# The local-attention loop of a two-block model on one core: three engines' order inside an iteration, and where the l2 norm's bound is applied

## The chip, the cores and the metric

One core of a Trainium2 chip runs the whole program. The engines each take their instructions in the order in which the program lists them, and wait for each other through semaphores: TensorE (PE in the profile, its weight loads apart as PEld), VectorE (DVE), ScalarE (ACT), GpSimd (POOL) and SyncE (SP), which here only issues DMAs. The metric is the device time of one launch in microseconds (us), the median of the runs.

## The reference, cut to what matters

The model takes `x` of 8 sequences x 256 tokens x 128 channels through ten residual steps. The change touches the two-layer local-attention block, which stands among them twice. All data is fp32.

```python
def _layer(x, wqkv, qs, ksc, wo, lg, lb, w1, b1, w2, b2):     # DIM 128, HEADS 8, DIM_HEAD 64, WINDOW 64
    h = shift_token(x)                                         # half of the channels from the token before
    q, k, v = jnp.split(h @ wqkv, 3, axis=-1)
    q, k, v = (to_heads(q), to_heads(k), to_heads(v))
    q = l2norm(q) * qs                                         # t / clip(norm(t), 1e-12)
    k = l2norm(k) * ksc
    q, k = rotary_xpos(q, k)
    o = local_attention(q, k, v)                               # own window and the one before, softmax
    x = x + o.transpose(0, 2, 1, 3).reshape(b, n, INNER) @ wo
    h = shift_token(x)
    h = (h - mu) / jnp.sqrt(var + 1e-05) * lg + lb             # layer norm
    a, g = jnp.split(h @ w1 + b1, 2, axis=-1)                  # 2 x 341 hidden units
    h = a * jax.nn.gelu(g, approximate=False)
    return x + h @ w2 + b2
...
for l in range(2):
    x = _layer(x, wqkv[l], q_scale[l], k_scale[l], wo[l], ...)
...
x = x + _L1_ffn_ref(_layernorm(x, axis=-1), ...)               # stands twice, with _L1_attn_b_ref between
```

## The kernel before, in words

A batch is 256 tokens, held as two tiles (`t` = 0, 1) of 128 tokens on the partitions. The local block is a loop over 2 layers x 8 batches, run twice (the first and the second block below). One iteration, `win(n, l, i)`, does three things at once: the attention of batch `i` (four units `u` of 64 query tokens and all 8 heads), the projections of the next batch (`nxt`: queries, keys, their rotation and norms, values), and pieces of the MLP of earlier batches (`hid` is batch i-1, whose layer norm is made, `m` is batch i-2, whose two matmul stages are made). The first two iterations of a block have no `m`, the first no `hid` either; the last has no `nxt`. So a block has 2 light iterations, 13 full ones with `nxt`, and the last. In the first block's second layer the iterations with `m` also normalise the finished batch for the next step (`fin`: `final_stats`, `norm_apply`); the second block needs no such norm.

Each engine's part of `win` is one list written by hand, and that list is what the engine does in order. The steps that the prediction follows:

- PE: `transpose_x` (the next batch's shifted tokens, which POOL copied to `xst`), `project_qk(t)` (queries and keys of tile t into two banks), `hidden_gates`, `hidden_values`, `hidden_out` (MLP), `local_scores(u)`, `transpose_probs(u)`, `weigh_values(u)`, `project_values(t)`, `transpose_qk(t)`, and `project_out`, the last step.
- ACT: `shifted` (the transposed tokens to `hT`), `gelus` between two table switches (`prime`), `squares(t)`, `local_exp(u)`, copies out of PSUM.
- DVE: `attn_max(u)`, `weigh(u)` (a reciprocal and a product), `rope_part(t, m)` (rotation of the queries, m = 0, and the keys, m = 1; the last one of a tile releases POOL's sum), `norms(t)` (sum of squares per head, then a `tensor_scalar` that bounds it from below by 1e-24), `hidden_stats` (mean and variance for the layer norm, ending in the small `tensor_scalar` at L1089 that writes `hvar`), `hidden_apply` (four `tensor_scalar`s of 128x64, L1096 and L1097), `gated`, `mlp_end`, `scaled(t)` (rotated values times the inverse norm, L999), and `local_residual`, which waits for `project_out`.
- POOL, unchanged in its order by the diff: `stage_copy` (L548, writes `xst`), the rotation's sum of tile 0 (L556, 128x1024), the inverse norms of tile 0 (L552, a power), `hidden_rstd`, with `m` in layer 1 `final_add`, the sum and the inverse norms of tile 1, and with `fin` the `final_rstd`, before the next `stage_copy`.

Of the kernel before, what the change touches and what calls it, by code (L numbers as in the profile page):

```python
# [26 lines left out]
P = 128  # L27
# [62 lines left out]
def attn_unit(u, groups):  # L90

    if u < groups:
# [29 lines left out]
        "dve_chain": F_UNITS, "ssq_chain": NT, "stage_ready": 1, "xT_psum": 1, "xT_ready": 1, "qk_psum": NT, "sq_ready": NT,  # L123
# [94 lines left out]
def build(nc, x, out, consts, w, plan):  # L218
    with ExitStack() as ctx:
# [242 lines left out]
        def _(pool):  # L462
# [68 lines left out]
            for n, kind in enumerate(plan):  # L531
# [22 lines left out]
                def rope_pool(v, i, t):  # L554
                    pool.wait_ge(sems["rope_ready"], v.at("rope_ready", i, t + 1))
                    pool.tensor_tensor(t1[:, t], t1[:, t], t2[:, t], ALU.add).then_inc(sems["rope_sum"], 1)  # L556
                    inverse_norms(v, i, t)

# [11 lines left out]

                def local_step(n, l, i):
                    _, nxt, m, hid = around(n, l, i)
                    fin = m and m[0] is vals[n + 3]
                    if nxt:
                        stage_copy(nxt[1], n + 2 * nxt[2])
                        rope_pool(nxt[0], nxt[1], 0)
# [4 lines left out]
                    if nxt:  # L581
                        rope_pool(nxt[0], nxt[1], 1)
# [81 lines left out]
        def _(dve):  # L664
# [323 lines left out]
            def norms(v, i, t, ch):  # L988

                dve.wait_ge(sems["sq_ready"], v.at("sq_ready", i, t + 1))
                ch.link(dve.tensor_reduce(ssq[:, t], sq[:, t].rearrange("p (h d) -> p h d", d=FHD), AX.X, ALU.add))
                dve.tensor_scalar(ssq[:, t], ssq[:, t], 1e-24, None, ALU.max).then_inc(sems["ssq_ready"], 1)  # L993

            def scaled(v, i, t):
# [3 lines left out]
                dve.tensor_tensor(qk[:, t].rearrange("p (h d) -> p h d", d=FHD), t1[:, t].rearrange("p (h d) -> p h d", d=FHD),  # L999
                                  inv[:, t].broadcast_to([P, 16, FHD]), ALU.mult).then_inc(sems["qk_ready"], 1)  # L1000

            def win_open(v, l, t):

                norms(v, 0, t, Chain(dve, v, "ssq_chain", 0, t))
# [8 lines left out]
            def win(n, l, i):  # L1013
# [4 lines left out]
                if nxt:  # L1018
                    vn, ni, nl = nxt
                    sch = Chain(dve, vn, "ssq_chain", ni)  # L1020
# [20 lines left out]
                weigh(0)  # L1041
                if m:
                    gated(*m)
# [4 lines left out]
                if m:  # L1048
# [1261 lines left out]
```

## Time and profile before

| | |
|---|---|
| median of 3 runs | 1893.99 us (1893.68 to 1896.01) |
| the profiled execution | 1894.08 us; from its first to its last instruction 1891.9 us |
| busy share of that span | PE 84%, DVE 70%, PEld 67%, ACT 59%, POOL 24% |
| granted TensorE clock, mean | 0.925 of full speed |
| first block's loop | 615.12 to about 1068 us |
| second block's loop | 1438.92 to about 1885 us |

An engine's busy share is an average over stages that have different limits. An iteration of the loop begins where PE transposes the staged tokens (line 2041 of the kernel before), so two starts of that line give its length.
### The profile page before, as it was taken

To read this page: it belongs to the slowest core of one execution; us is meant where nothing else is said; L and a number is where in the kernel's file an instruction comes from. 1 tells how busy PE (TensorE), PEld (TensorE's weight loads), DVE (VectorE), ACT (ScalarE), POOL (GpSimd) and SP (SyncE) were. 2 spreads that over 40 slices of the span, in tenths; PEclk is the share of its full clock that TensorE was granted. 3 is DMA by queue.
4 is the path that set the end of the run, shared out by engine and by line. 5 is a ranking of instruction groups with operands and counts; after the bars stand their busy time and mean duration, and the time that the engine had idled before them with its cause. 6 is when DMAs were issued, how large, how long until landed. Compare 5 with 4: busy or idle time off the path is not lost.

```text
span 1891.9 us, 31365 instructions
## 1 busy us (share of the span) xinstructions
PE 1587.9 (84%) x9787; PEld 1268.3 (67%) x9787; DVE 1333.8 (70%) x3495; ACT 1116.8 (59%) x2975; POOL 454.2 (24%) x342
## 2 busy tenths in 40 slices
PE   6999989766555789889878799999986889888986
PEld 5888888334344567776667677777764667766775
DVE  4678877788985777877776555565646877887783
ACT  2355455233221788888777743443425888888885
POOL 1110010000002443434444100000004443434450
PEclk9999999677677999999999999998998999999999
DMA  4000000000010000000000000000000000000000
GB/s 144 1 1 0 0 0 1 1 1 1 1 56 0 2 4 3 1 4 4 2 3 1 4 1 0 0 0 0 0 1 1 4 3 3 2 4 4 3 1 25
DMA packets 15110, 13.49 MB, mean 7 GB/s; under 512 B 11286, under 2 KB 14266, under 8 KB 14650
## 3 DMA queue, kind: packets, MB, share of 16 engines
q1 hardware_dynamic: 15034, 12.55, 2.1%
q8 instruction: 38, 0.62, 0.1%
q14 instruction: 38, 0.31, 0.1%
HBM read 9.41 MB, written 1.05 MB: 6 GB/s over the span
## 4 chain that ended last, share of the span: by engine, by line
PE 59%; DVE 18%; issue 11%; ACT 9%; POOL 2%; DVEq 0%; POOLq 0%; ACTq 0%
PE bank L1740 5%; PE bank L1715 5%; PE bank L1752 4%; PE bank L1681 4%; PE bank L1701 4%; PE bank L1879 3%; PE bank L1727 3%; PE bank L1766 3%; PE bank L1861 2%; DVE arena_ffn L984 2%; PE bank L1883 2%; PE bank L1692 2%; PE bank L1899 2%; PE bank L1956 2%; DVE hvar L1089 2%
## 5 line engine op out<-in xcount | busy, mean ns | idle before, releaser
L556 POOL TENSOR_TENSOR arena_ffn<-arena_ffn 128x1024 f32<-128x1024 f32 x60 | 141.5, 2358 | 397.3 <-DVE arena_ffn L984 397.3
L552 POOL TENSOR_TENSOR inv<-ssq,mhalf 128x16 f32<-128x16 f32 x64 | 188.1, 2940 | 67.9 <-DVE ssq L993 64.4
L1437 ACT ACTIVATE bank<-bank,nmaxF 128x128 f32<-128x128 f32 x512 | 173.3, 340 | 49.7 <-DVE nmaxF L717 48.9
L1367 ACT ACTIVATE prob<-bank,nmax 128x128 f32<-128x128 f32 (+1 forms) x256 | 90.1, 420 | 114.9 <-DVE nmax L717 90.5
L1715 PEld LDWEIGHTS bank<-arena_setup 128*128 128x128 f32 x1024 | 146.1, 206 | 10.2 <-issue 1.3
L1727 PE MATMUL bank<-ident,prob 128*128 128x128 f32 x512 | 83.9, 290 | 79.9 <-DVE prob L1028 55.0
L1727 PEld LDWEIGHTS bank<-ident,prob 128*128 128x128 f32 x512 | 63.1, 148 | 122.8 <-issue 100.9
L1715 PE MATMUL bank<-arena_setup 128*128 128x128 f32 x1024 | 145.2, 288 | 0.0
L540 POOL TENSOR_TENSOR rstd<-var,mhalf 128x2 f32<-128x2 f32 x24 | 17.0, 709 | 524.2 <-DVE var L679 524.2
L1752 PE MATMUL bank<-packF,hT 128*128 128x512 f32 x256 | 130.9, 637 | 11.5 <-DVE arena_ffn L984 9.8
L717 DVE TENSOR_REDUCE nmaxF<-bank 128x4 f32<-128x512 f32 x128 | 88.4, 691 | 70.2 <-PE bank L1715 70.1
L1388 ACT ACT_TABLE_LOAD x91 | 116.8, 1283 | 1.6
L980 DVE TENSOR_TENSOR arena_ffn<-bank,rope 128x512 f32<-128x512 f32 x128 | 87.5, 683 | 32.2 <-ACT arena_attn L1415 32.2
L1740 PE MATMUL bank<-probT,vF 128*128 128x128 f32 x768 | 101.9, 282 | 4.7 <-ACT probT L1444 4.3
L1437 ACT ACTIVATION_READ_ACCUMULATOR bank<-bank,nmaxF 128x1 f32 x512 | 105.2, 205 | 0.4
L1456 ACT ACTIVATE arena_setup<-bank 64x256 f32<-64x256 f32 x256 | 96.2, 376 | 10.7 <-PE bank L1740 9.1
L1681 PE MATMUL bank<-arena_attn 128*128 128x256 f32 (+1 forms) x512 | 100.0, 328 | 0.0
L1841 PE MATMUL bank<-xqT,w1s 128*114 128x256 f32 (+1 forms) x384 | 97.3, 390 | 1.8 <-ACT arena_forget L1475 0.7
L1740 PEld LDWEIGHTS bank<-probT,vF 128*128 128x128 f32 x768 | 90.7, 191 | 11.8 <-issue 6.9
L984 DVE TENSOR_TENSOR arena_ffn<-bank,rope 128x256 f32<-128x256 f32 x256 | 95.4, 414 | 0.0
L1141 DVE TENSOR_TENSOR arena_forget<-bank,maskG 128x384 f32<-128x384 f32 x128 | 68.1, 552 | 38.5 <-PE bank L1901 35.0
L1415 ACT ACTIVATE arena_attn<-bank 128x512 f32<-128x512 f32 x128 | 69.5, 599 | 43.1 <-PE bank L1752 43.1
(271 smaller groups left out, 4128.3 us busy)
## 6 DMA issues: line engine op xcount, KB each, us to landing
packF<-in_packF SPq DMA_DIRECT2D x1, 3122.0 KB
arena_history<-in_packG SPq DMA_DIRECT2D x1, 2560.0 KB, 9.8
HS<-XH SPq DMA_DIRECT2D x32, 63.5 KB
X<-in_x_tiled SPq DMA_DIRECT2D x1, 1024.0 KB, 4.9
out_dram<-X SPq DMA_DIRECT2D x8, 128.0 KB, 1.9
arena_setup<-in_const_masks_a SPq DMA_DIRECT2D x1, 512.0 KB, 5.5
HS<-XH SPq DMA_DIRECT2D x32, 0.2 KB
arena_setup<-in_const_rope SPq DMA_DIRECT2D x1, 256.0 KB
```

The source lines that it names most:

```text
L552: pool.tensor_tensor(inv[:, t, :, 0], ssq[:, t, :, 0], mhalf[:, 0:16], ALU.pow).then_inc(sems["inv_ready"], 1)
L556: pool.tensor_tensor(t1[:, t], t1[:, t], t2[:, t], ALU.add).then_inc(sems["rope_sum"], 1)
L984: ins = dve.tensor_tensor(heads(t2[:, t, cols])[:, :, d], a[:, :, e], tab, ALU.mult)
L1388: act.activation(primer[:, col:col + 1], mhalf[:, 0:1], func)
L1437: ins = act.activation(cols, cols, ACT.Exp, bias=nmaxF[:, u, c:c + 1], accum_out=denF[:, u, c])
L1456: ins = act.activation(yTF[rows_, u // 2, :, 64 * (u % 2):64 * (u % 2) + 64], bank[6 + u % 2][rows_].rearrange("p (c j k) -> p c j k", j=2 ...
L1681: ins = pe.matmul(bank[s % banks][:, n * width:(n + 1) * width], q, k, start=False, stop=True, skip_group_check=True)
L1715: ins = pe.matmul(b[:, c * P:(c + 1) * P].rearrange("p (a k) -> p a k", a=2), qZ[:, u, c].rearrange("p j k -> p (j k)"), kT[:, c, F_KEYS[u ...
L1727: ins = pe.transpose(bank[4 + u % 2][:, c * P:(c + 1) * P], prob[:, u % 2, c * P:(c + 1) * P], ident[:])
L1740: ins = pe.matmul(bank[6 + u % 2][:, c * P:(c + 1) * P], values[:, c * P:(c + 1) * P], probT[:, u % 2, c * P:(c + 1) * P], start=True, sto ...
L1752: ins = pe.matmul(bank[banks[m]][:], hT[:, t * P:(t + 1) * P], f_at[f"wqkv{l}"][:, 512 * m:512 * m + 512], start=True, stop=True)
L1841: return pe.matmul(dst, w1s[:, l, lo:lo + n], xqT[:], start=True, stop=True)
```

## The change

The bound moves: `norms` no longer has the `tensor_scalar` that bounds the sum of squares, and `scaled` becomes a `scalar_tensor_tensor` that bounds the inverse norm from above by 1e12 in the same pass. The remaining edits give the engines' steps in an iteration another order. POOL's functions are split in two, with the same order of instructions.

```diff
             def norms(v, i, t):
                 dve.wait_ge(sems["sq_ready"], v.at("sq_ready", i, t + 1))
-                ch.link(dve.tensor_reduce(ssq[:, t], sq[:, t].rearrange("p (h d) -> p h d", d=FHD), AX.X, ALU.add))
-                dve.tensor_scalar(ssq[:, t], ssq[:, t], 1e-24, None, ALU.max).then_inc(sems["ssq_ready"], 1)
+                dve.tensor_reduce(ssq[:, t], sq[:, t].rearrange("p (h d) -> p h d", d=FHD), AX.X, ALU.add).then_inc(sems["ssq_ready"], 1)
...
-                dve.tensor_tensor(qk[:, t].rearrange("p (h d) -> p h d", d=FHD), t1[:, t].rearrange("p (h d) -> p h d", d=FHD),
-                                  inv[:, t].broadcast_to([P, 16, FHD]), ALU.mult).then_inc(sems["qk_ready"], 1)
+                dve.scalar_tensor_tensor(qk[:, t].rearrange("p (h d) -> p h d", d=FHD), inv[:, t].broadcast_to([P, 16, FHD]), 1e12,
+                                         t1[:, t].rearrange("p (h d) -> p h d", d=FHD), ALU.min, ALU.mult).then_inc(sems["qk_ready"], 1)
...
+                scaled(v, i, 1)
                 attn_max(v, i, 0, 4, P, nmaxF, F_SCORE_BANKS)
-                scaled(v, i, 1)
                 if nxt:
                     rope_part(vn, ni, nl, 0, 0)
-                attn_max(v, i, 1, 4, P, nmaxF, F_SCORE_BANKS)
-                if nxt:
-                    rope_part(vn, ni, nl, 0, 1)
+                if m:
+                    gated(*m)
                 if hid:
                     hidden_stats(*hid)
                 if nxt:
-                    norms(vn, ni, 0, sch)
+                    rope_part(vn, ni, nl, 0, 1)
+                attn_max(v, i, 1, 4, P, nmaxF, F_SCORE_BANKS)
                 weigh(0)
+                if nxt:
+                    norms(vn, ni, 0)
                 if m:
-                    gated(*m)
+                    mlp_end(m[0], m[1])
                 weigh(1)
...
                 weigh(3)
-                if nxt:
-                    norms(vn, ni, 1, sch)
                 if hid:
                     hidden_apply(*hid)
                 if nxt:
-                    scaled(vn, ni, 0)
-                local_residual(v, i, l)
+                    norms(vn, ni, 1)
                 if fin:
                     final_stats(m[0], m[1])
+                if nxt:
+                    scaled(vn, ni, 0)
+                if fin:
                     norm_apply(m[0], m[1])
+                local_residual(v, i, l)
...
                 if m:
                     prime(ACT.Gelu)
+                    gelus(*m)
                 if nxt:
                     squares(vn, ni, 0)
                 if m:
-                    gelus(*m)
                     prime(ACT.Exp, 1)
                 local_exp(v, i, 0)
+                middle_values(v, i)
                 take_qkT(v, i, 1)
                 local_exp(v, i, 1)
...
                     transpose_x(vn, ni, bank[2])
-                local_scores(v, i, 0)
-                if nxt:
-                    project_qk(vn, ni, nl, 0)
                 if m:
                     hidden_gates(*m, 0)
                     pe.wait_ge(sems["down_used"], v.at("down_used", i, 0))
                     hidden_gates(*m, 1)
-                local_scores(v, i, 1)
+                if nxt:
+                    project_qk(vn, ni, nl, 0)
+                local_scores(v, i, 0)
                 if m:
                     hidden_values(*m)
                 transpose_qk(v, i, 1)
+                local_scores(v, i, 1)
+                if m:
+                    hidden_out(*m)
                 if nxt:
                     project_qk(vn, ni, nl, 1)
+                local_scores(v, i, 2)
                 transpose_probs(v, i, 0)
-                local_scores(v, i, 2)
-                if m:
-                    hidden_out(*m)
                 local_scores(v, i, 3)
                 transpose_probs(v, i, 1)
```

The lists of PE and ACT also change near the end of an iteration (`project_values(1)` earlier, `weigh_values(3)` behind the hidden transpose, one copy of ACT's moved).

DVE, the end of a full iteration (the batch before the last of layer 0), before: `weigh(3)`, then the sum of squares and its bound, `hidden_apply` on `hn`, the scaling and the residual.

```order
L980 TENSOR_TENSOR arena_ffn<-bank,rope 128x512
L984 TENSOR_TENSOR arena_ffn<-bank,rope 128x8x32 x2
L1025 RECIPROCAL rdenF<-denF 128x4
L1028 TENSOR_TENSOR prob<-bank,rdenF 128x512
L992 TENSOR_REDUCE ssq<-arena_attn 128x16
L993 TENSOR_SCALAR ssq<-ssq 128x16
L1096 TENSOR_SCALAR hn<-XH,mv,hrstd 128x64
L1097 TENSOR_SCALAR hn<-HS,mv,hrstd 128x64
L1096 TENSOR_SCALAR hn<-XH,mv,hrstd 128x64
L1097 TENSOR_SCALAR hn<-HS,mv,hrstd 128x64
L999 TENSOR_TENSOR arena_attn<-arena_ffn,inv 128x1024
L1071 TENSOR_TENSOR XH<-XH,bank 128x256
```

The same place now.

```order
L981 TENSOR_TENSOR arena_ffn<-bank,rope 128x512
L985 TENSOR_TENSOR arena_ffn<-bank,rope 128x8x32 x2
L1024 RECIPROCAL rdenF<-denF 128x4
L1027 TENSOR_TENSOR prob<-bank,rdenF 128x512
L1094 TENSOR_SCALAR hn<-XH,mv,hrstd 128x64
L1095 TENSOR_SCALAR hn<-HS,mv,hrstd 128x64
L1094 TENSOR_SCALAR hn<-XH,mv,hrstd 128x64
L1095 TENSOR_SCALAR hn<-HS,mv,hrstd 128x64
L993 TENSOR_REDUCE ssq<-arena_attn 128x16
L999 SCALAR_TENSOR_TENSOR arena_attn<-inv,arena_ffn 128x1024
L1069 TENSOR_TENSOR XH<-XH,bank 128x256
```

`hidden_apply` has moved ahead of the sum of squares, the bound has gone, and the scaling stands right behind the sum of squares.

PE, the start of a full iteration of the rolled loop, before (`xst` is the staged batch, `hT` its transposed tokens, `xqT` the MLP's input):

```order
L2041 MATMUL bank<-ident,xst 128x128
L2042 MATMUL bank<-ident,xst 128x128
L1712 MATMUL bank<-maskFb,identb 128x512
L1715 MATMUL bank<-arena_setup 128x128 x4
L1752 MATMUL bank<-packF,hT 128x512 x2
L1841 MATMUL bank<-xqT,w1s 114x256 x2
L1841 MATMUL bank<-xqT,w1s 113x256
```

The same place now.

```order
L2040 MATMUL bank<-ident,xst 128x128
L2041 MATMUL bank<-ident,xst 128x128
L1840 MATMUL bank<-xqT,w1s 114x256 x2
L1840 MATMUL bank<-xqT,w1s 113x256
L1750 MATMUL bank<-packF,hT 128x512 x2
L1710 MATMUL bank<-maskFb,identb 128x512
L1713 MATMUL bank<-arena_setup 128x128 x4
```

The gates of the MLP now stand between the transposes and the projection, and the scores of unit 0 behind the projection.

## Rows read from the trace of the kernel before

**Rows 1.** Loop stretches: us, busy (x instructions) of PE, PEld, DVE, ACT, POOL; clock, DMA.

```profile
615.12:668.09 52.97, 42.37 (x263) 32.19 (x263) 36.75 (x74) 39.90 (x124) 23.34 (x11) 0.94 0.01 2
668.09:887.27 219.18, 196.79 (x1250) 156.39 (x1249) 170.17 (x384) 188.30 (x545) 92.43 (x48) 0.98 0.01 3
887.27:1061.84 174.57, 145.58 (x900) 117.36 (x898) 124.92 (x316) 136.29 (x399) 65.98 (x41) 0.94 0.01 3
1491.77:1818.31 326.54, 292.93 (x1875) 232.29 (x1873) 255.07 (x576) 282.49 (x817) 141.53 (x76) 0.98 0.01 3
```

**Rows 2.** PE in time order, one full iteration: start, duration, line [idle before <-releaser].

```profile
1709.35 0.27 PE L2041 MATMUL bank<-ident,xst 128*128 128x128 f32 x1
...
1710.98 1.89 PE L1752 MATMUL bank<-packF,hT 128*128 128x512 f32 x4
...
1715.10 1.46 PE L1841 MATMUL bank<-xqT,w1s 128*114 128x256 f32 x6
...
1721.99 0.65 PE L1727 MATMUL bank<-ident,prob 128*128 128x128 f32 x4 [2.70 <-DVE prob L1028]
...
1734.48 1.95 PE L1773 MATMUL bank<-packF,arena_setup 128*128 128x128 f32 x16
1736.26 0.27 PE L2041 MATMUL bank<-ident,xst 128*128 128x128 f32 x1
```

**Rows 3.** DVE in time order, the same iteration.

```profile
1717.18 0.22 DVE L1082 BATCH_NORM_STATS2 stats<-XH 128x6 f32 x1
...
1718.28 1.43 DVE L1089 TENSOR_SCALAR hvar<-mv 128x2 f32<-128x2 f32 x1 [0.17 <-DVE mv L1087]
1719.62 1.21 DVE L992 TENSOR_REDUCE ssq<-arena_attn 128x16 f32<-128x1024 f32 x1
...
1721.78 1.26 DVE L1110 SCALAR_TENSOR_TENSOR arena_forget<-bank,b1s,arena_forget 114x256 f32<-114x256 f32 x3
1722.96 0.17 DVE L1025 RECIPROCAL rdenF<-denF 128x4 f32<-128x4 f32 x1
...
1723.79 0.69 DVE L717 TENSOR_REDUCE nmaxF<-bank 128x4 f32<-128x512 f32 x1
1724.40 0.68 DVE L980 TENSOR_TENSOR arena_ffn<-bank,rope 128x512 f32<-128x512 f32 x1
...
1725.66 0.41 DVE L1116 TENSOR_TENSOR XH<-XH,bank 128x256 f32 x1
...
1731.39 0.30 DVE L1096 TENSOR_SCALAR hn<-XH,mv,hrstd 128x64 f32 x1
...
1732.28 1.21 DVE L999 TENSOR_TENSOR arena_attn<-arena_ffn,inv 128x1024 f32<-128x1024 f32 x1
```

**Rows 4.** POOL in time order, the same iteration.

```profile
1717.34 2.35 POOL L556 TENSOR_TENSOR arena_ffn<-arena_ffn 128x1024 f32<-128x1024 f32 x1 [9.45 <-DVE arena_ffn L984]
...
1731.55 2.91 POOL L552 TENSOR_TENSOR inv<-ssq,mhalf 128x16 f32<-128x16 f32 x1
1734.42 0.40 POOL L548 COPY xst<-XH 128x256 f32 x1
```

**Rows 5.** All engines in time order, the head of a `fin` iteration.

```profile
948.01 0.33 PE L2041 MATMUL bank<-ident,xst 128*128 128x128 f32 x1 [2.65 <-POOL xst L548]
```

**Rows 6.** All engines in time order, just behind the first block's loop.

```profile
1077.31 0.72 POOL L565 TENSOR_TENSOR X<-X,XH 128x256 f32<-128x256 f32 x1
1077.37 0.71 DVE L1096 TENSOR_SCALAR hn<-XH,mv,hrstd 128x64 f32<-128x64 f32 x1 [0.59 <-POOL hrstd L561]
```

**Rows 7.** All engines in time order, end of the first block's first iteration.

```profile
637.07 1.21 DVE L999 TENSOR_TENSOR arena_attn<-arena_ffn,inv 128x1024 f32<-128x1024 f32 x1
637.23 3.82 POOL L552 TENSOR_TENSOR inv<-ssq,mhalf 128x16 f32<-128x16 f32 x1
```

**Rows 8.** All engines in time order, an earlier stage of the program.

```profile
265.16 1.04 POOL L520 TENSOR_TENSOR taps<-ident,arena_setup 128x512 f32<-128x512 f32 x1
265.26 0.24 DVE L793 RECIPROCAL qrecip<-qscale 128x16 f32<-128x16 f32 x1
```

More of the change, by code:

```diff
@@ L122 @@
     "win": {
-        "dve_chain": F_UNITS, "ssq_chain": NT, "stage_ready": 1, "xT_psum": 1, "xT_ready": 1, "qk_psum": NT, "sq_ready": NT,
+        "dve_chain": F_UNITS, "stage_ready": 1, "xT_psum": 1, "xT_ready": 1, "qk_psum": NT, "sq_ready": NT,
         "v_psum": NT, "v_ready": NT,
@@ L569, in final_rstd, with rope_sum @@
                     pool.tensor_tensor(rstd[:], var[:], mhalf[:, 0:NT], ALU.pow).then_inc(sems["rstd_ready"], 1)
+                def rope_sum(v, i, t):
+                    pool.wait_ge(sems["rope_ready"], v.at("rope_ready", i, t + 1))
+                    pool.tensor_tensor(t1[:, t], t1[:, t], t2[:, t], ALU.add).then_inc(sems["rope_sum"], 1)
                 def local_step(n, l, i):
-                    _, nxt, m, hid = around(n, l, i)
+                    v, nxt, m, hid = around(n, l, i)
                     fin = m and m[0] is vals[n + 3]
@@ L575, in local_step @@
                         stage_copy(nxt[1], n + 2 * nxt[2])
-                        rope_pool(nxt[0], nxt[1], 0)
+                        rope_sum(nxt[0], nxt[1], 0)
+                        inverse_norms(nxt[0], nxt[1], 0)
                     if hid:
@@ L581, in local_step @@
                     if nxt:
-                        rope_pool(nxt[0], nxt[1], 1)
+                        rope_sum(nxt[0], nxt[1], 1)
+                        inverse_norms(nxt[0], nxt[1], 1)
                     if fin and m[0] is not vals[-1]:
@@ L986, in rope_part, with norms @@
                     ins.then_inc(sems["rope_ready"], 1)
-            def norms(v, i, t, ch):
+            def norms(v, i, t):
                 dve.wait_ge(sems["sq_ready"], v.at("sq_ready", i, t + 1))
-                ch.link(dve.tensor_reduce(ssq[:, t], sq[:, t].rearrange("p (h d) -> p h d", d=FHD), AX.X, ALU.add))
-                dve.tensor_scalar(ssq[:, t], ssq[:, t], 1e-24, None, ALU.max).then_inc(sems["ssq_ready"], 1)
+                dve.tensor_reduce(ssq[:, t], sq[:, t].rearrange("p (h d) -> p h d", d=FHD), AX.X, ALU.add).then_inc(sems["ssq_ready"], 1)
             def scaled(v, i, t):
@@ L1047, in win @@
                     rope_part(vn, ni, nl, 1, 0)
-                if m:
-                    mlp_end(m[0], m[1])
                 attn_max(v, i, 3, 4, P, nmaxF, F_SCORE_BANKS)
@@ L1498, in win @@
                     squares(vn, ni, 1)
-                middle_values(v, i)
+                probs_copy(v, i, 0)
                 local_exp(v, i, 2)
-                probs_copy(v, i, 0)
                 probs_copy(v, i, 1)
@@ L1506, in win @@
                 take_yT(v, i, 1)
+                take_yT(v, i, 2)
                 probs_copy(v, i, 3)
-                take_yT(v, i, 2)
                 if hid:
@@ L1820, in win @@
                     project_values(vn, ni, nl, 0)
+                weigh_values(v, i, 2)
                 transpose_probs(v, i, 3)
-                weigh_values(v, i, 2)
-                weigh_values(v, i, 3)
+                if nxt:
+                    project_values(vn, ni, nl, 1)
                 if hid:
@@ L1826, in win @@
                     transpose_hidden(hid[0], hid[2])
+                weigh_values(v, i, 3)
                 if nxt:
-                    project_values(vn, ni, nl, 1)
                     transpose_qk(vn, ni, 0)
```

10 lines of the change are left out of this document (1 added, 9 removed).

## The prediction

> **What bounds the kernel now.** I read the windows of the loop first, then PE, DVE and POOL in time order over one iteration, then the places elsewhere in the trace where POOL and DVE overlap. By the windows the loop makes an iteration in about 27 us: eight full ones take 219.18, twelve take 326.54, the two light ones at a block's head 52.97, and the stretch with `fin` 174.57 [rows 1]. A full iteration in which nothing slows TensorE lasts from 1709.35 to 1736.26, 26.91 us [rows 2]. 8 x 26.91 = 215.3 and 12 x 26.91 = 322.9, so 3.9 and 3.6 us are left, with the granted clock at 0.98 in both windows. The only pause of PE in [rows 2] that is longer than about a microsecond is the 2.70 ahead of the first transposes of probabilities, and I take the falls of the clock to come behind it.
>
> That pause ends with `weigh(0)` on DVE. [Rows 3] show what DVE did before: the small `hvar` instruction on 128x2 took 1.43, and then the sum of squares took 1.21. The 1.43 isn't its own work. POOL's sum of tile 0 ran from 1717.34 for 2.35, to 1719.69 [rows 4], and `hvar` ended at 1719.71. So a `tensor_scalar` on DVE that comes under POOL's 128x1024 sum is held until that sum ends. The same is seen on the form of `hidden_apply`: 0.71 instead of 0.30 under a POOL addition of 0.72 that had begun 0.06 earlier [rows 6, 3]. It also goes the other way: POOL's power, 2.91 alone [rows 4], takes 3.82 when it is issued 0.16 behind the scaling on DVE, 0.91 more [rows 7]. But a scaling that starts when the power already runs is not held: 1.21 at 1732.28, inside the power of 1731.55 [rows 3, 4]. There are 28 such scalings, all 1.21.
>
> At the end PE is the last: the staged copy is done at 1734.82 [rows 4], the output projection runs from 1734.48, and the next iteration starts at 1736.26 [rows 2]. In a `fin` iteration it is the other way, PE waits 2.65 for the copy [rows 5], because POOL must first make the final norm's power.
>
> **The change part by part.** Times below count from PE's start of the iteration.
>
> *Head.* On PE the same three steps (projection, gates, scores) stand ahead of the second rotation, in another order. In [rows 2] they take 15.10 - 10.98 = 4.12. With the two transposes (0.22, an estimate from the 0.27 of one) the scores of unit 0 are ready at about 4.5, and `attn_max(0)` ends at 5.15, which is the first thing that DVE has to wait for; the ACT squares, no longer behind two table switches, are ready at about 4.9 by my walk.
>
> *DVE from there runs without a pause.* Start to start in [rows 3]: a rotation 1.26 (24.40 to 25.66), the gated product 1.18 (21.78 to 22.96), `weigh` 0.83 (22.96 to 23.79), a maximum 0.61 (23.79 to 24.40), the sum of squares 1.21, `mlp_end` 0.41, the statistics 1.10 with `hvar` at 0.1 now that POOL's sum isn't running. `hvar` comes ahead of the second rotation, so POOL's sum starts behind it: 1.3 saved. Until the last rotation releases POOL's second sum DVE does four rotations (5.04), the product (1.18), the statistics (1.2), three maxima (1.83), three weighings (2.49), one sum of squares (1.21) and `mlp_end` (0.41): 13.4, so 18.5.
>
> *The tail, where it is lost again.* POOL's sum runs 18.5 to 20.85 (2.35, [rows 4]). DVE does `weigh(3)` and issues `hidden_apply` at 19.3. Before, the sum of squares stood there and hid POOL's sum; now four `tensor_scalar`s come under it, and by the 1.43 and the 0.71 the first is held to 20.85: 1.5 lost where `hvar` gained 1.3. The other three take 0.22 each ((32.28 - 31.39)/4 in [rows 3]) and end at 21.5. The sum of squares ends at 22.7. The bound that is gone would have been 0.2 to 0.3 here. `scaled(0)` needs nothing that is late, so DVE issues it at 22.65, just ahead of the power at 22.75: that is the arrangement of [rows 7], so the power takes 3.82 and not 2.91, to 26.5. The copy (0.40, [rows 4]) ends at 26.9. PE: scaling ends 23.8, eight transposes about 0.9 (half of the sixteen matmuls of 1.79 between 1734.48 and 1736.26), the projection 1.79: 26.5. So the copy becomes last, at 26.9: a full iteration keeps its 26.9. The bound's own 0.2 goes to nothing: it lay on DVE ahead of a power that now starts no earlier.
>
> The scaling as one `scalar_tensor_tensor` has no row of its own size. Below, it costs the 1.21 of the product; above, the L1110 form costs 0.39 per 256 columns start to start, 1.57 for 1024 columns. I take 1.21; +0.36 on PE's path would still end at 26.9.
>
> *What is gained.* (a) The 2.70 pause: `weigh(0)` now stands ahead of the sum of squares, and `hidden_out` and the second projection stand in PE's list before the transposes. By the walk PE's longest pauses are about 1.1. If the falls of the clock go with the pause, the 3.9 and the 3.6 go, and 1.4 in the rest: -9. (b) `fin` iterations: the final statistics (about 1.0, like `hidden_stats`) now stand between the sum of squares and the scaling, so the power starts alone and takes 2.91: 25.65, the final power 0.7 (an estimate between 0.40 and 2.91), copy 0.40: 26.75. PE: scaling 1.0 later, 24.8, transposes 0.9, projection 1.79: 27.4. Before, the five of them with projections take 30.5 each (174.57 less 22 for the last batch's part, by five): -3.1 each, -15.5, and some 1.5 of the last batch's: -17. (c) Light iterations: 52.97 for two. The same walk without the product and `mlp_end` is 1.6 shorter, 25.3; without the statistics (1.2) and the held `hidden_apply` too, the first would be 23 or 24, where PE's and ACT's own steps bind. Together 49.2, -3.7 in each block. As I can't walk the waits for ACT well there, I take -3 in each: -6.
>
> Sum: 0 - 9 - 17 - 6 = -32. The profiled execution's own time is 1894.08, the median of the runs 1893.99, so 0.1 between them. 1894 - 32 = **1862**.
>
> A rule speaks against part (b). The row is the 1.21 of the scaling inside the running power [rows 3, 4]. The Trainium skill, page "SBUF — State Buffer", section "Who interferes with whom", says that VectorE and GpSimd share one pair of ports as an exclusive lock, that a VectorE instruction with two SBUF inputs contends with a GpSimd instruction that reads SBUF, and that whichever was issued first makes the other wait. The trace agrees for the 1.43, the 0.71 and the 3.82, but not for the 1.21, where the rule would have it wait.
>
> **The rivals.**
>
> 1. *The clock falls as often as before.* The new pauses of about 1.1 would do what the 2.70 did. The light windows, at 0.94, speak for it. Then (a) and about half of (b) and (c) are gone: -10 - 3, 1881.
>
> 2. *The tail isn't held.* If `hidden_apply` under the sum, or the power under the scaling, runs at its own length, the period is 1.5 or, with PE last at 26.5, 0.4 shorter. For `hidden_apply` with 27 iterations: -40 more, 1822. The 1.43 and 0.71 speak against.
>
> 3. *The scaling waits for the power in `fin`.* If the scaling, issued 0.9 behind the power, waited for its end, it would start 2.0 later: 2.0 x 6 = 12, 1874. The 28 rows of 1.21 are against it. This is what the Trainium skill's rule above would make; by the row the sum stays 1862.
>
> 4. *The other side: reciprocals are held.* `weigh(0)` begins with a reciprocal (0.17), and now stands 0.6 behind the second rotation, that is inside POOL's first sum. The reciprocal at 265.26 took 0.24 inside a POOL addition of 1.04 [rows 8], so I take it that this form isn't held. If it is, each of 30 iterations with a next batch loses 2.35 - 0.61 = 1.74 on DVE's unbroken chain: +52, 1914. It decides once it is held for over 1.1 us, since 30 x 1.1 covers the 32.
>
> 5. *Nothing.* The order only moves the waits about: 1894. The period of a full iteration, unchanged in my sum, speaks for it, the 2.65 of [rows 5] against.
>
> **How the numbers follow.** The likeliest case has 0.58, and its own range is 1846 to 1876: 26 iterations times 0.5 us of error in the period is 13. Rival 1 has 0.14, rival 2 0.08, rival 3 0.06, rival 4 0.09, rival 5 0.05. Leaving out rivals 2 and 4 and the half of 5 that lies above, the range is **1836 to 1885**. A measurement of this kernel can tell about 0.2% (3.8 us) from no change. Faster: 0.58 + 0.14 + 0.08 + 0.06 = 0.86; same 0.05; slower 0.09.
>
> **What would show it.** In the changed profile: `hvar` at about 0.2; the first instruction of `hidden_apply` at about 1.7, ending with POOL's second sum; the power of tile 1 at 3.8 in full and 2.9 in `fin` iterations; the head of a full iteration waiting for the copy by 0.3 to 0.5; no pause of PE over 1.5 inside; starts 26.9 apart, 27.4 with `fin`; the granted clock at 1.00 in most full iterations. I'm wrong if the first rotation doesn't start by 5.2, if DVE pauses between it and the last one (then a full iteration is longer by each pause), or if the clock falls in the short pauses.

## The result, and the profile after

The changed kernel takes 1887.55 us (median of 7 runs, 1878.80 to 1887.90) against 1896.01 of the kernel before, a ratio of 0.9942 (95% interval 0.9924 to 0.9960). It is faster, but by 8 us and not by 32, and the time lies outside the range. A second timing gave 0.9914 (e2).

The windows of the changed kernel, stage by stage (the stretch, its length, then busy time of PE, PEld, DVE, ACT and POOL, the granted clock, DMA): all that stands ahead of the loop; the first block's light iterations, its eight full ones, those with `fin` and the last; the stages between the blocks; the second block's light iterations and twelve of its full ones; its last two iterations and the end.

```profile
0.00:622.61 622.61, 477.70 (x2753) 387.91 (x2754) 462.02 (x1245) 228.54 (x567) 70.60 (x117) 0.84 0.05 16
622.61:675.39 52.78, 42.92 (x264) 32.20 (x263) 33.70 (x70) 40.47 (x124) 24.27 (x11) 0.96 0.01 2
675.39:890.07 214.68, 197.56 (x1249) 153.94 (x1249) 163.44 (x369) 189.26 (x544) 99.63 (x48) 1.00 0.01 3
890.07:1051.43 161.36, 143.23 (x918) 114.15 (x919) 122.34 (x316) 138.38 (x399) 66.63 (x43) 0.99 0.01 3
1051.43:1436.14 384.71, 350.40 (x2133) 280.96 (x2132) 209.72 (x713) 151.80 (x266) 20.23 (x25) 0.91 0.00 0
1436.14:1491.01 54.87, 44.56 (x265) 32.31 (x263) 33.80 (x70) 41.82 (x125) 24.27 (x11) 0.94 0.01 2
1491.01:1812.94 321.93, 296.46 (x1872) 230.73 (x1873) 245.12 (x553) 283.72 (x816) 152.28 (x76) 1.00 0.01 3
1812.94:1885.40 72.46, 55.81 (x340) 43.68 (x340) 37.55 (x99) 46.19 (x134) 16.34 (x11) 0.93 0.06 17
```

Of the kernel before, the stretches that [rows 1] don't hold, from a second execution of it (e1):

```profile
0.00:615.30 615.30, 471.44 (x2754) 380.01 (x2755) 460.78 (x1246) 228.74 (x567) 70.79 (x117) 0.85 0.05 16
887.40:1066.60 179.20, 148.50 (x920) 119.76 (x918) 126.55 (x326) 138.63 (x402) 67.04 (x43) 0.94 0.01 3
1066.60:1439.10 372.50, 337.85 (x2133) 270.19 (x2133) 209.32 (x716) 151.13 (x264) 20.26 (x25) 0.95 0.00 0
1818.50:1892.10 73.60, 55.74 (x342) 44.55 (x340) 38.50 (x101) 46.37 (x135) 15.48 (x11) 0.93 0.06 17
```

Read together with [rows 1], this is the whole balance. In the loop the full iterations become shorter by 4.5 (214.68 against 219.18) and 4.6 (321.93 against 326.54) with the clock now at 1.00, the `fin` stretch by 17.8 (161.36 against 179.20, the clock 0.99 against 0.94, so a part of this is the clock's), the light ones by 0.2 in the first block, while those of the second become 2.0 longer (54.87 against 52.85, from 1438.92 to 1491.77 in the first trace of before): -25.1. The last stretch, which holds the second block's last two iterations, gives 1.1 more: -26.2. Outside the loop 7.3 are added ahead of it and 12.2 between the blocks: +19.5. The diff touches next to nothing there (the bound of the norms that open a block is gone, which makes the last step ahead of the loop 0.4 shorter, 21.75 against 22.16). Between the blocks the same number of matmuls (x2133) runs at a lower clock (0.91 against 0.95). -26.2 + 19.5 = -6.7, the difference of the two spans (1885.4 and 1892.1).

Inside an iteration the walk of the prediction can be laid on the trace. VectorE of the changed kernel in time order, the iteration that starts at 755.81:

```profile
761.01 0.68 DVE L981 TENSOR_TENSOR arena_ffn<-bank,rope 128x512 f32<-128x512 f32 x1
...
764.41 0.17 DVE L1087 TENSOR_SCALAR hvar<-mv 128x2 f32<-128x2 f32 x1
...
766.35 0.17 DVE L1024 RECIPROCAL rdenF<-denF 128x4 f32<-128x4 f32 x1
...
774.76 1.76 DVE L1094 TENSOR_SCALAR hn<-XH,mv,hrstd 128x64 f32 x1
...
777.11 1.21 DVE L993 TENSOR_REDUCE ssq<-arena_attn 128x16 f32<-128x1024 f32 x1
778.24 1.21 DVE L999 SCALAR_TENSOR_TENSOR arena_attn<-inv,arena_ffn 128x1024 f32<-128x1024 f32 x1
```

POOL in the same iteration:

```profile
765.91 2.35 POOL L568 TENSOR_TENSOR arena_ffn<-arena_ffn 128x1024 f32<-128x1024 f32 x1 [10.16 <-DVE arena_ffn L985]
...
774.11 2.35 POOL L568 TENSOR_TENSOR arena_ffn<-arena_ffn 128x1024 f32<-128x1024 f32 x1 [2.09 <-DVE arena_ffn L985]
778.39 3.82 POOL L552 TENSOR_TENSOR inv<-ssq,mhalf 128x16 f32<-128x16 f32 x1 [1.93 <-DVE ssq L993]
782.17 0.39 POOL L548 COPY xst<-XH 128x256 f32 x1
```

PE, the start that follows:

```profile
782.62 0.33 PE L2040 MATMUL bank<-ident,xst 128*128 128x128 f32 x1 [0.24 <-POOL xst L548]
```

`hvar` takes 0.17 instead of the 1.43 of [rows 3]. The hold has gone to `hidden_apply`: 774.76 + 1.76 = 776.52, and POOL's second sum, issued at 774.11, ends at 776.46. The power is issued 0.15 behind the scaling and takes 3.82, as in [rows 7]. The reciprocal at 766.35 lies inside POOL's first sum and isn't held. PE waits 0.24 for the copy and starts 26.81 behind the last start. In a `fin` iteration the power runs first, and the scaling inside it isn't held either:

```profile
967.16 2.91 POOL L552 TENSOR_TENSOR inv<-ssq,mhalf 128x16 f32<-128x16 f32 x1 [1.93 <-DVE ssq L993]
...
967.89 1.23 DVE L999 SCALAR_TENSOR_TENSOR arena_attn<-inv,arena_ffn 128x1024 f32<-128x1024 f32 x1
```

What remains to be found is the 19.5 us outside the loop.

### The profile page after: what moved, and what is told of

Its sections match the earlier page's. It is cut to its first block, busy times and chain, and to the rows that moved or that the text cites. A ratio compares the mean times of both kernels' runs of the same rounds, so it can differ in the third digit from the quotient of the medians.

```text
span 1885.4 us, 31303 instructions
## 1 busy us (share of the span) xinstructions
PE 1608.7 (85%) x9787; PEld 1275.9 (68%) x9787; DVE 1307.7 (69%) x3431; ACT 1120.2 (59%) x2975; POOL 474.2 (25%) x342
## 4 chain that ended last, share of the span: by engine, by line
PE 44%; DVE 28%; issue 16%; ACT 6%; POOL 5%; DVEq 1%; POOLq 0%; ACTq 0%
DVE arena_ffn L985 4%; PE bank L1679 4%; PE bank L1699 4%; PE bank L1750 3%; PE bank L1878 3%; DVE arena_ffn L981 3%; DVE nmaxF L718 3%; POOL arena_ffn L568 3%; PE bank L1840 2%; PE bank L1898 2%; PE bank L1690 2%; PE bank L1882 2%; DVE ssq L993 2%; PE bank L1955 2%; PE bank L1921 2%
## 5 line engine op out<-in xcount | busy, mean ns | idle before, releaser
L552 POOL TENSOR_TENSOR inv<-ssq,mhalf 128x16 f32<-128x16 f32 x64 | 209.2, 3268 | 83.2 <-DVE ssq L993 83.2
L1750 PE MATMUL bank<-packF,hT 128*128 128x512 f32 x256 | 129.8, 632 | 34.5 <-DVE arena_ffn L985 25.8
L1713 PEld LDWEIGHTS bank<-arena_setup 128*128 128x128 f32 x1024 | 136.7, 194 | 23.7 <-issue 19.6
L1713 PE MATMUL bank<-arena_setup 128*128 128x128 f32 x1024 | 136.7, 277 | 0.0
L1738 PE MATMUL bank<-probT,vF 128*128 128x128 f32 x768 | 107.5, 283 | 2.2 <-ACT probT L1442 0.7
L1750 PEld LDWEIGHTS bank<-packF,hT 128*128 128x128 f32 x256 | 47.5, 197 | 77.5 <-issue 33.9
L1699 PEld LDWEIGHTS bank<-vaug,probT 128*128 128x128 f32 x768 | 96.7, 196 | 0.7 <-DVE probT L725 0.3
L1764 PE MATMUL bank<-packF,hT 128*128 128x512 f32 x128 | 72.0, 649 | 28.1 <-DVE arena_ffn L985 28.0
L718 DVE TENSOR_REDUCE nmax<-bank 128x2 f32<-128x512 f32 (+1 forms) x96 | 66.1, 688 | 42.5 <-PE bank L1679 41.3
```

The lines of the kernel that those rows point to most:

```text
L552: pool.tensor_tensor(inv[:, t, :, 0], ssq[:, t, :, 0], mhalf[:, 0:16], ALU.pow).then_inc(sems["inv_ready"], 1)
L718: dve.tensor_reduce(out_[:, u, 0:heads], bank[u % banks][:, 0:heads * keys].rearrange("p (h k) -> p h k", k=keys), AX.X, ALU.max, negate=T ...
L1699: ins = pe.matmul(o, probT[:, u % 2, n * P:(n + 1) * P], val, start=first, stop=(kt == keys // P - 1), skip_group_check=True)
L1713: ins = pe.matmul(b[:, c * P:(c + 1) * P].rearrange("p (a k) -> p a k", a=2), qZ[:, u, c].rearrange("p j k -> p (j k)"), kT[:, c, F_KEYS[u ...
L1738: ins = pe.matmul(bank[6 + u % 2][:, c * P:(c + 1) * P], values[:, c * P:(c + 1) * P], probT[:, u % 2, c * P:(c + 1) * P], start=True, sto ...
L1750: ins = pe.matmul(bank[banks[m]][:], hT[:, t * P:(t + 1) * P], f_at[f"wqkv{l}"][:, 512 * m:512 * m + 512], start=True, stop=True)
```

## The experiments

A fall of the clock means below that the granted clock goes to its lower level, 1.2 GHz, for some time. The theories of the 19.5 are these. A: which pauses of TensorE bring a fall depends on where they lie in time, so that a loop of another length sets the falls of the next stage otherwise. B: a program's falls are fixed by its instructions, the same in each execution. C: the denser loop itself makes the clock fall more behind it. A further question is which edits carry the gain in the loop. A loop's length is told below as the sum of two stretches: the first block from its first start to the start of the next stage, and the second from its first start to the start of its last full iteration (the changed kernel: 428.8 and 376.8, 805.6; before: 830.7).

**e1 and e2: both kernels unchanged.**

> The kernel before, unchanged, to see a second execution of it in the trace. Theory A (the clock's falls outside the local loop depend on how the pauses of TensorE lie against the clock's own grid, which is another one in each execution): the grid's offset is another than 0.77 us, and the stages outside the loop, together 1061 us in the first trace, differ by several us from it, with falls at other places; the loop itself stays within 2 us of 451 and 379. Theory B (a program's falls are fixed by its instructions): the same falls at the same places as in the first trace, each stage within 1 us.

> The changed kernel, unchanged. Theory A: loop 429 and 377 us again (full iterations 26.8, with the final norm 27.25), and the stages outside differ from the 1080 us of the first trace; the 85.5 us stage between 1331 and 1416 and the 155.9 us of the early stage come out otherwise. Theory B: 85.5 and 155.9 again. Both: the median some 8 us under the kernel before, since seven runs showed that.

e1: 1894.22 us, and every stage within 0.2 us of the first trace. The clock's first rise came at nearly the same time in both (24.8 and 24.7 us), so this run can't tell A from B. e2: 1880.75 us (8 runs, ratio 0.9914, 0.9878 to 0.9951), loop 805.8. Its head, the part ahead of the loop, took 618.50 and not 622.61, so what is lost there isn't the same in each execution. But the end of the part between the blocks has the same long fall in both. The changed kernel, two pauses of PE on the same line there:

```profile
1329.96 0.70 PE L1898 MATMUL bank<-arena_setup 64*128 64x256 f32 x4 [1.78 <-DVE arena_forget L1139]
...
1370.23 0.92 PE L1898 MATMUL bank<-arena_setup 64*128 64x256 f32 x4 [1.79 <-DVE arena_forget L1139]
```

The window from the first pause to the second and one from the second on, then the whole of what the expectations call the last eighth, from the last start of a batch there to the start of the next stage:

```profile
1329.96:1370.23 40.27, 38.25 (x258) 31.14 (x258) 23.49 (x83) 17.73 (x31) 0.77 (x2) 1.00 0.00 0
1370.23:1404.25 34.02, 32.66 (x153) 29.04 (x153) 17.09 (x65) 0.00 (x0) 0.00 (x0) 0.51 0.00 1
1330.81:1416.30 85.49, 77.57 (x452) 66.44 (x451) 41.65 (x155) 20.11 (x35) 2.09 (x4) 0.77 0.00 0
```

The window behind the same pause in e2, and its last eighth:

```profile
1366.31:1400.53 34.22, 32.86 (x152) 29.17 (x153) 17.11 (x65) 0.00 (x0) 0.00 (x0) 0.50 0.00 1
1326.90:1412.60 85.70, 77.76 (x453) 66.62 (x452) 41.67 (x155) 20.13 (x35) 2.10 (x4) 0.77 0.00 0
```

The last eighth of the kernel before (e1):

```profile
1347.30:1419.80 72.50, 64.14 (x453) 54.76 (x452) 41.60 (x155) 20.12 (x35) 2.10 (x4) 0.95 0.00 0
```

Behind the pause at 1370.23 the clock is at its lower level (1.2 GHz) for 34 us, although PE is busy for 32.66 of them; behind the pause 40.27 earlier, as long (1.78), it stays at 2.4 GHz. The kernel before does this stretch in 72.5. So the last eighth is 13 us longer with this fall in it. Theory B fails for the head. From the loop on the two executions have the same falls, and the traces point to the reason: in both the clock rises out of the head's last fall 0.4 us behind the loop's first start (0.43 to 0.47 in all ten traces here with the bound moved, 0.04 to 0.05 in the four with it in place), so from there on each execution of one kernel begins alike against the clock.

**e5, e6 and e11: a delay in front of that stage.** The same edit in the changed kernel with 8 and 16, and in the kernel before with 8:

```diff
                 settle()
+                for k in range(pads):
+                    dve.bn_stats(padding[:, k], XH[:, i, 0, 0:64])
...
-                    hidden_stats(vm, vals[n + 2], NB - 1)
+                    hidden_stats(vm, vals[n + 2], NB - 1, 8)
```

> The changed kernel with eight more statistics instructions (0.13 us each start to start, into a tile that nothing reads) on VectorE's path just behind the first block's loop, where TensorE waits for it: the stage behind begins about 1.0 us later against the loop, and nothing else changes. Theory A (where the loop's end puts the pauses of 1.8 us of the next stage decides which of them bring a long fall of the clock): the falls in the stage behind come at other pauses; the last eighth of it, 85.5 and 85.7 us in both executions of the changed kernel, is 71 to 76 in this one or in the next, and the kernel becomes faster by up to 13 us although work was added. Theory C (the denser loop itself brings the falls): 85 again, and the kernel 1 us slower than with the change.

> The same with sixteen such instructions, about 2.1 us. Theory A: again other pauses, and the last eighth of the stage at 71 to 76 in at least one of the two kernels. Theory C: 85 again, 2 us slower than with the change.

> The kernel before with the eight statistics instructions of e5 at the same place, about 1.0 us. Theory A: the falls in the stage behind the first loop move to other pauses, and the last eighth of it, 72.5 in both executions of before, may come out at another of the lengths seen (71 to 90); the total is not 1.0 us longer but anything from 3 us shorter to 14 longer. Theory C (the changed loop brings the falls): the stage is as before, total +1.0.

e5: 1875.27 us (ratio 0.9888, 0.9855 to 0.9920). e6: 1870.26 us (0.9873, 0.9843 to 0.9904). PE's wait there grows from 3.00 to 4.00 and 5.02, the loops are those of the changed kernel (805.3 and 805.2), and with work added the kernels are faster than the changed one. In e5 the head is that of the changed kernel's first trace (622.6 in both), and 10.0 of the 10.3 us between the two spans lie between the blocks. The last eighth in e5:

```profile
1331.10:1406.40 75.30, 66.99 (x452) 56.86 (x450) 41.58 (x154) 20.13 (x35) 2.10 (x4) 0.91 0.00 0
```

e6, from the pause at the same place on (here it was 1.43 and brought no fall), the last eighth, and the whole part between the blocks:

```profile
1365.54:1385.71 20.17, 18.02 (x152) 16.13 (x153) 17.01 (x65) 0.00 (x0) 0.08 (x1) 1.00 0.01 2
1326.50:1398.90 72.40, 64.08 (x452) 54.67 (x450) 41.55 (x155) 20.12 (x35) 2.10 (x4) 0.95 0.00 0
1043.30:1418.10 374.80, 338.55 (x2133) 270.49 (x2132) 211.62 (x729) 151.87 (x266) 20.24 (x25) 0.95 0.00 1
```

The same 152 matmuls take 20.17 instead of 34.02 (x153), and the part between the blocks 374.80 instead of 384.71, with 2 us more work in it. Theory C fails: the loop is as dense as in the changed kernel. In e11 (1901.39, ratio 1.0022, 0.9987 to 1.0057, no change that can be told) the falls moved to other places (1227.3 and 1312.6 us instead of 1178.4 and 1301.2), as A says. The part between the blocks took 375.9, 3.4 more, where C told 1.0 more. The last eighth stayed at 72.4, so of that stretch e11 shows nothing; its head took 623.1.

The traces bear A out from another side. Take the time from the clock's last rise to the start of the second batch of that stage, and count the stage's later falls from that start. In the kernel before it is 15.0 us (the start is at 1097.79), in e6 15.0 too (1077.19), and the falls come at the same places in both, 80.6, 203.5 and 309.3 us on, with the same last eighth (72.46 and 72.44). The first two in the kernel before:

```profile
1178.40:1185.20 6.80, 6.80 (x26) 5.72 (x26) 2.81 (x10) 1.24 (x2) 0.00 (x0) 0.50 0.00 0
1301.20:1311.40 10.20, 10.20 (x42) 8.58 (x42) 3.98 (x13) 2.35 (x4) 0.00 (x0) 0.50 0.00 0
```

The first two in e6:

```profile
1157.80:1164.60 6.80, 6.80 (x26) 5.69 (x26) 2.80 (x10) 1.26 (x2) 0.00 (x0) 0.50 0.00 0
1280.70:1290.90 10.20, 10.20 (x42) 8.58 (x41) 3.86 (x13) 2.48 (x4) 0.00 (x0) 0.50 0.00 0
```

In e4, e5 and e8, three kernels with different loops, that time is 14.1, and all three have their first falls at 160.0 and at 245.3 or 245.4. So the falls go with where the stage starts against the clock's changes, and not with the kind of loop ahead of it. It doesn't fix everything: at 16.5 the changed kernel and e11 both have their first fall at 120.0, but it lasts 6.8 us in the one and 10.2 in the other, and from there on they differ. e9, at 14.0, also leaves the others behind its first fall. Why isn't shown.

**e4, e8 and e9: the two smallest parts in the kernel before.** e4 has the edit of `norms` and `scaled` alone. e8 has this alone, e9 both:

```diff
                 attn_max(v, i, 1, 4, P, nmaxF, F_SCORE_BANKS)
+                if hid:
+                    hidden_stats(*hid)
                 if nxt:
                     rope_part(vn, ni, nl, 0, 1)
-                if hid:
-                    hidden_stats(*hid)
```

> The kernel before with only the bound moved; the order of all engines as before. By the walk of the prediction the 0.5 us of the bound lies on VectorE ahead of hidden_apply and of the scaling for which TensorE waits at the end of a full iteration: 26.9 becomes 26.45, with the final norm 0.4 less, together -12 us: 1884. If the bound was hidden (the prediction gave it nothing in the changed order): 1894 to 1896. hvar stays at 1.4 and the pause of 2.7 stays, so the clock falls in every third full iteration as before.

> The kernel before with one edit: VectorE's hidden_stats ahead of the second rotation instead of behind it. If the hold of hvar under POOL's first sum is the loss that the change repaired: hvar 0.17 instead of 1.43, the pause ahead of the first transposes of probabilities 1.4 instead of 2.7, and, as hidden_apply still stands behind the sum of squares, an iteration 25.6 to 26.2 instead of 26.9 and without the fall in every third: 30 to 45 us faster than the kernel before, about as fast as e3. If the whole new order is needed: within 10 us of the kernel before, with the falls still there.

> The kernel before with the two edits of e4 and e8 together: the bound moved, and hidden_stats ahead of the second rotation. In e8 the hold passed on to the next small instruction, the bound of tile 0 (1.30 instead of 0.17), in e4 hvar kept it. If one hold that needs some small tensor_scalar to sit under POOL's first sum is the whole loss: with neither there, the pause ahead of the first transposes is under 0.5, a full iteration 25.7 and without falls, the loop 35 to 45 us shorter than before, and no edit of TensorE's or ScalarE's order is needed for it. If the new order of TensorE and ScalarE carries the gain: a full iteration 26.5 to 27.0.

e4: 1892.84 us (0.9986, 0.9962 to 1.0009), loop 827.6: 3 less, and not 12. An undisturbed iteration took 26.6 (26.45 expected), but now every second iteration took 28.2 instead of every third, with the clock at 0.97 in eight iterations. Most of what the bound gave, the clock took. e8: 1885.92 (0.9957, 0.9941 to 0.9973), loop 819.8. The falls in the full iterations are gone, but an iteration takes 27.0, and the expectation of 25.6 to 26.2 failed, and with it the 30 to 45 us. The pause ahead of the first transposes of probabilities, 2.70 before, in e4 and in e8:

```profile
1583.62 0.65 PE L1723 MATMUL bank<-ident,prob 128*128 128x128 f32 x4 [2.48 <-DVE prob L1026]
```

```profile
1553.70 0.65 PE L1727 MATMUL bank<-ident,prob 128*128 128x128 f32 x4 [1.36 <-DVE prob L1028]
```

VectorE and POOL of e8:

```profile
1548.89 0.17 DVE L1089 TENSOR_SCALAR hvar<-mv 128x2 f32<-128x2 f32 x1
...
1551.47 1.30 DVE L993 TENSOR_SCALAR ssq<-ssq 128x16 f32<-128x16 f32 x1
```

```profile
1550.39 2.35 POOL L556 TENSOR_TENSOR arena_ffn<-arena_ffn 128x1024 f32<-128x1024 f32 x1 [10.87 <-DVE arena_ffn L984]
```

The hold has passed on to the next `tensor_scalar` in the list, the bound of tile 0: 1551.47 + 1.30 = 1552.77, POOL's sum ends at 1552.74. With both edits no `tensor_scalar` is left under POOL's first sum: e9 takes 1844.02 us (0.9721, 0.9693 to 0.9749), its loop 783.2. The parts alone gave 3.1 and 10.9 of the loop, together they give 47.5. Full iterations of e9 in the first block (eight):

```profile
669.00:872.70 203.70, 192.08 (x1251) 152.88 (x1251) 156.87 (x368) 187.04 (x545) 91.77 (x48) 1.00 0.01 3
```

VectorE, POOL and PE in the one that starts at 720.01, where most of the sum of squares and all of the reciprocal now lie inside POOL's sum (729.42 to 731.78) and run at their own length, and PE's longest pause is 1.29:

```profile
729.25 1.21 DVE L992 TENSOR_REDUCE ssq<-arena_attn 128x16 f32<-128x1024 f32 x1
730.38 0.17 DVE L1023 RECIPROCAL rdenF<-denF 128x4 f32<-128x4 f32 x1
```

```profile
729.42 2.36 POOL L556 TENSOR_TENSOR arena_ffn<-arena_ffn 128x1024 f32<-128x1024 f32 x1 [10.91 <-DVE arena_ffn L984]
```

```profile
729.39 1.98 PE L1748 MATMUL bank<-packF,hT 128*128 128x512 f32 x4 [1.29 <-DVE arena_ffn L984]
```

No edit of PE's or ACT's lists is in e9. Its 25.5 an iteration is less than the changed kernel's 26.8.

**e3, e7, e10 and e12: single steps of the changed kernel.** e3:

```diff
-                if hid:
-                    hidden_apply(*hid)
                 if nxt:
                     norms(vn, ni, 1)
+                if hid:
+                    hidden_apply(*hid)
```

> The changed kernel with the four small instructions of hidden_apply behind the sum of squares instead of ahead of it, so that the sum of squares lies under POOL's second sum and nothing is held. If the hold (1.76 instead of 0.30) is what keeps a full iteration at 26.8: the first hidden_apply instruction under 0.7, the power 2.9, an iteration 25.9, with the final norm 26.4, the loop 25 us shorter than with the change. If something else of TensorE or ScalarE binds there: 26.5 or more. Theory A: the median follows the loop, about 1862, give or take 8. A rival theory C (what the loop gains is taken back outside it by the clock): the median stays at 1880 to 1888.

1843.26 us (0.9724, 0.9685 to 0.9763), loop 777.6, 28.0 less than with the change; an iteration 25.9, 26.1 with `fin`. VectorE and POOL in one of them:

```profile
765.75 0.65 DVE L1094 TENSOR_SCALAR hn<-XH,mv,hrstd 128x64 f32 x1
...
766.98 1.21 DVE L999 SCALAR_TENSOR_TENSOR arena_attn<-inv,arena_ffn 128x1024 f32<-128x1024 f32 x1
```

```profile
766.30 2.91 POOL L552 TENSOR_TENSOR inv<-ssq,mhalf 128x16 f32<-128x16 f32 x1
```

One exchange of two steps takes away most of the hold (0.65 instead of 1.76, where 0.30 is the instruction's own) and the power's 0.91 (2.91 instead of 3.82). The time fell by 37 to 44 us against the two medians of the changed kernel, more than the loop's 28 and below the 1862, give or take 8, that was expected. In the traces the rest is 8.5 between the blocks (376.2 against 384.7; the last eighth took 71.4) and 6.3 in the head (616.3 against 622.6).

e7 puts one step of PE back in the light iterations, e10 does so in e3 for a block's first iteration alone (`hid` instead of `m`):

```diff
+                if not m:
+                    local_scores(v, i, 0)
                 if nxt:
                     project_qk(vn, ni, nl, 0)
-                local_scores(v, i, 0)
+                if m:
+                    local_scores(v, i, 0)
```

> The changed kernel with one step of TensorE's list back in its old place in the light iterations alone: the scores of unit 0 ahead of the projection. The prediction gave each light iteration 3 us less and they took 27.2, 25.6, 27.7 and 27.2. If the loss there is TensorE's wait for the transposed tokens (2.15 and 1.19 us ahead of the projection, which the scores used to fill): the wait falls to 1.1 or less, the four light iterations take 25 to 26, together 5 to 8 us less. If the rotation's chain on VectorE binds instead: no change in the four, less than 1 us in all.

> e3 with the scores of unit 0 ahead of the projection in the first iteration of a block alone (in e7 it took 2.3 and 1.3 off that one and gave it back in the next, by a pause of 3.5). By the loop: 3 to 4 us less than e3, 1839. Theory A: the stage behind may take that back or add to it by where its pauses then lie, 1833 to 1850.

The waits of the changed kernel in its two light iterations:

```profile
625.38 2.72 PE L1750 MATMUL bank<-packF,hT 128*128 128x512 f32 x4 [2.15 <-ACT hT L1408]
...
651.36 1.98 PE L1750 MATMUL bank<-packF,hT 128*128 128x512 f32 x4 [1.19 <-ACT hT L1408]
```

e7: 1882.98 us (0.9940, 0.9919 to 0.9962), loop 803.3. The first light iteration of a block takes 24.9 and 26.3 instead of 27.2 and 27.7, so the wait for ACT was a loss there; the second takes 27.3 and 27.1 instead of 25.6 and 27.2, in the first block with a pause of 3.48 ahead of the second projection. Together the four take 2.1 less, not the 5 to 8 expected. Its last eighth took 89.7. e10: 1855.13 us (0.9778, 0.9749 to 0.9807), slower than e3 by 12 (by 6.9 in the two traces) although its loop, 776.0, is 1.6 shorter; its last eighth:

```profile
1308.60:1394.20 85.60, 77.67 (x453) 66.51 (x452) 41.64 (x155) 20.12 (x35) 2.09 (x4) 0.77 0.00 0
```

That is the long fall again, in a kernel that differs from e3 by one step on PE in a block's first iteration. Theory A has it that this can happen, but the time is above the 1850 that the expectation gave as its upper end.

> The changed kernel with the final statistics behind the scaling of tile 0 instead of ahead of it. If what stands between the sum of squares and the scaling decides whether POOL's power is held: the power in the iterations with the final norm takes 3.82 instead of 2.91, PE's start waits for the copy, and these iterations take 27.9 to 28.2 instead of 27.25. If not: 27.25, with the power at 2.91.

e12 (the two steps `final_stats` and `scaled(vn, ni, 0)` exchanged): 1877.46 us in one run. The power took 3.82, as expected, but the iterations with `fin` took 27.5 and not 27.9 to 28.2:

```profile
967.73 3.82 POOL L552 TENSOR_TENSOR inv<-ssq,mhalf 128x16 f32<-128x16 f32 x1 [1.93 <-DVE ssq L993]
```

In the changed kernel the copy there was done by 971.1 and PE started at 971.9, a margin of 0.8, so that most of the 0.9 by which the power is longer doesn't show: the iteration is 0.2 longer (27.47 against 27.25).

## Why the prediction was wrong, point by point

- *The tail of a full iteration.* Right in each piece, or nearly: `hidden_apply` held (1.7 told, 1.76), the power 3.8 (3.82), PE waiting 0.3 to 0.5 for the copy (0.24), an iteration 26.9 (26.81). e3 shows that these two losses are what kept it there: without them it takes 25.9.
- *(a), the clock in the full iterations, -9.* The two windows gave 9.1 (4.5 and 4.6), clock 1.00. Of this 7.1 is the clock (3.9 and 3.6 were left over before, 0.2 and 0.2 are now), the rest is the iteration's 0.1, twenty times. Rival 1 is out for the full iterations: PE's pauses of 0.7 brought no fall there. In the light ones the clock is still at 0.96 and 0.94, but their pauses are longer (2.15 and 2.56 in the first block). e4 and e8 bear out that the 2.70 pause had brought the falls: with 2.48 left they came more often, with 1.36 none.
- *(b), `fin`, -17.* -17.8; an iteration takes 27.25 where 27.4 was told. The scaling inside the running power isn't held (1.23), against the rule weighed there and rival 3.
- *(c), light iterations, -6.* Failed: +1.8. The walk left out that the gates which fill PE's wait for the transposed tokens are missing in them, while the scores that filled it before now stand behind the projection (2.15 and 1.19). e7 gives back 2.1 of the 7.8 by putting them ahead of it; where the rest goes isn't shown as a whole. In the second light iteration PE also waits 2.56 for a rotation ahead of the second projection.
- *The bound's own 0.2 "goes to nothing".* No run has the changed order with the bound left in it, so this isn't shown. What the runs show is its worth in the order before: little alone (3.1 of the loop, e4), and 36.6 once `hidden_stats` stands ahead of the rotation (e8 to e9), since in e8 the bound had become the held instruction, which the prediction hadn't considered.
- *Rivals 2, 4 and 5.* Out: 1.76 and 3.82 are holds, and the reciprocal inside the sum took 0.17. The total comes near rival 5, but not by its reason: the loop did become 26 us shorter.
- **The step that failed** is the sum: "0 - 9 - 17 - 6 = -32", taken off 1894 as if the rest of the program kept its time. That term stood at nothing without a reason, and it measured +19.5. The loop gave -26.2, with (c) mis-sized by 7.8. Of the 19.5, 12.2 lie between the blocks. That they come from where the falls lie, and not from the denser loop, is shown by e5 and e6, where a delay gave back 10 of them. The 7.3 ahead of the loop aren't the change's doing. What the diff does there makes the head 0.4 shorter, and over the fourteen executions traced here the head goes with the time of the clock's first rise, whichever the kernel: 613.9 to 615.3 us where that comes at 23.9 to 24.8 (six traces, the kernel before, e6 and e10 among them), 618.5 at 25.0 (e2), 622.6 to 623.1 at 25.7 to 25.9 (the changed kernel's first trace, e5, e12 and e11, whose loop and head are those of the kernel before), 616.3 to 616.9 at 26.2 to 26.7 (e3, e4 and e8).

That the second timing of the changed kernel, 1880.75, lies inside the range is luck and no support for the sum. Behind the head its two traces take the same, 1262.8 and 1262.9, so a head that varies by 9 us is enough for the spread of all its timings (1878.80 to 1887.90). That it is the reason stays argued: of a timed run that isn't the profiled one the stages aren't recorded.

The clock went by what was told in the loop and by something else outside: the same pause at the same line left it at 1.00 in one batch and at 0.51 in the next. The Trainium skill, page "TensorE: Matmul & The Clock Gate", section "What's actually happening", says that the look at TensorE's activity runs on a rhythm of its own, which doesn't start with the kernel. The traces agree in that the first rise came at 23.9 to 26.7 us of the program, and that the head, with the same instructions, differed by up to 9 us between executions (613.9 in e10, 622.8 in e12).

## What to carry to other kernels

When a small instruction is held by another engine's large one, look at what stands behind it in the list: moving it alone hands the hold to the next of its kind, and the cure is to leave none of them under the large one (e8, e9, e3). Where TensorE's clock falls behind pauses, compare stages by their own windows before you believe a total: a saving of 26 us in the loop showed as 8, and an idle of 2 us as a gain of 10 or more. Such a gain is no property of the edit. The safer aim would be the pause that brings the fall; no run here tried it outside the loop.

## What the hardware showed that I hadn't expected

- A fall of the clock can outlast the pause by far: 34 us at 0.51 with PE busy for 32.66 of them, in a stretch whose 152 matmuls take 20.17 at full clock.
- `tensor_scalar` under POOL's 128x1024 sum is held to the sum's end at 128x2, 128x16 and 128x64 alike (1.43, 1.30, 1.76), while a reciprocal (0.17) and a sum of squares (1.21, e9) under that sum are not, nor is a `scalar_tensor_tensor` inside POOL's power (1.23).
- An iteration's falls come in step with the iterations: every third at 26.9, every second at 26.6 (e4), so that a saving of 0.3 each was given back for the most part.
- The same time since the clock's last rise gave a stage the same falls in kernels with different loops (before and e6; e4, e5 and e8), though not in every pair of traces (the changed kernel and e11).
